# The list of tokens read as one run per partition, its places worked out on VectorE

## The reference

```
x = x + cross_attention(layernorm(x), ctx)          # 1 head: own key and 77 outer keys
h = layernorm(x)
qkv  = h @ W_qkv + b_qkv                             # 16 heads of 32
attn = softmax(q k^T / sqrt(32)) v
gate = softmax(h @ W_gate + b_gate)                  # 8 experts
top_g, top_i = top_k(gate, 2)                        # two experts for each token
moe  = sum over the two of  top_g * (h @ W_experts[e] + b_experts[e])
x = x + attn + moe
```

## Time and profile before

| | us |
|---|---|
| median of 3 runs | 1365.55 |
| lowest, highest | 1362.95, 1366.89 |
| the profiled execution | 1362.68 |
| its span | 1361.0 |

### The profile page before, as it was taken

The page is one execution under the profiler, slowest core; times in us unless marked ns, Lnnn a source line. Parts: engine busy times, 40 slices in busy tenths (PEclk is TensorE's granted clock), DMA queues, the critical chain, the costliest instruction groups (busy, mean ns, idle before and its releaser), DMA issues.

```text
span 1361.0 us, 27015 instructions
## 1 busy us (share of the span) xinstructions
PE 1252.1 (92%) x7540; PEld 961.7 (71%) x7541; DVE 960.1 (71%) x2149; ACT 893.8 (66%) x1874; POOL 373.4 (27%) x580
## 2 busy tenths in 40 slices
PE   5928999999888899999999999999996999999997
PEld 4927888888666567767777677777774666787775
DVE  5517888888678888888888888888885673433332
ACT  3303444444348789999999999999995783334332
POOL 0002222222200011310213102130005174667775
PEclk9878999999899999999999999999999898999999
DMA  5055777777665247455674555744559677887874
GB/s 185 14 171 176 277 259 252 267 261 254 237 171 137 60 135 171 86 126 140 159 170 85 125 138 153 179 83 127 134 122 251 243 188 185 242 190 131 143 139 59
DMA packets 114301, 225.28 MB, mean 166 GB/s; under 512 B 27627, under 2 KB 35963, under 8 KB 111941
## 3 DMA queue, kind: packets, MB, share of 16 engines
q1 hardware_dynamic: 86517, 181.76, 44.4%
q0 software_dynamic: 26624, 42.04, 17.2%
q10 hardware_dynamic: 1104, 0.81, 0.2%
HBM read 89.72 MB, written 77.75 MB: 123 GB/s over the span
## 4 chain that ended last, share of the span: by engine, by line
PE 72%; DVE 7%; DMA 7%; ACT 5%; issue 4%; SPq 3%; another core or an unknown queue 1%; POOL 1%; POOLq 1%; DVEq 0%; ACTq 0%
PE banks L237 14%; PE banks L239 13%; PE banks L238 13%; PE banks L1241 8%; PE banks L1222 8%; PE banks L1200 7%; DMA out_dram<-plain,score_bias 4%; ACT plain L928 2%; ACT banks L921 2%; DVE plain L1761 2%; SPq L417 2%; PE banks L1330 1%; PE banks L1070 1%; PE banks L1108 1%
## 5 line engine op out<-in xcount | busy, mean ns | idle before, releaser
L237 PE MATMUL banks<-parts 128*128 128x512 f32 (+8 forms) x1036 | 418.4, 404 | 29.7 <-DVE parts L1542 7.4
L239 PE MATMUL banks<-parts 128*128 128x512 f32 (+8 forms) x1036 | 398.4, 385 | 0.0
L238 PE MATMUL banks<-parts 128*128 128x512 f32 (+8 forms) x1036 | 397.9, 384 | 0.0
L1761 DVE TENSOR_REDUCE plain<-banks 128x1 f32<-128x512 f32 x512 | 339.9, 687 | 72.8 <-PE banks L1200 54.8
L921 ACT ACTIVATE banks<-banks,plain 128x512 f32<-128x512 f32 x512 | 345.1, 679 | 15.5 <-DVE plain L1761 15.2
L928 ACT ACTIVATE plain<-banks 128x1024 f32<-128x1024 f32 x256 | 265.8, 1038 | 45.7 <-PE banks L1222 40.4
L237 PEld LDWEIGHTS banks<-parts 128*128 128x128 f32 (+2 forms) x1036 | 198.9, 192 | 79.0 <-issue 18.3
L239 PEld LDWEIGHTS banks<-parts 128*128 128x128 f32 (+2 forms) x1036 | 197.6, 191 | 39.1
L238 PEld LDWEIGHTS banks<-parts 128*128 128x128 f32 (+2 forms) x1036 | 199.0, 192 | 28.6
L1200 PE MATMUL banks<-parts 96*128 96x512 f32 x512 | 181.2, 405 | 0.2 <-issue 0.2
L1222 PE MATMUL banks<-parts 104*128 104x512 f32 x512 | 176.0, 425 | 2.6 <-ACT plain L928 2.6
(11 more groups left out here) (193 smaller groups left out, 1532.0 us busy)
## 6 DMA issues: line engine op xcount, KB each, us to landing
parts<-parts SPq DMA_DIRECT2D x385, 128.0 KB, 2.4
parts<-h_turned SPq DMA_DIRECT2D x46, 512.0 KB, 6.2
experts_split<-parts SPq DMA_DIRECT2D x32, 512.0 KB, 4.1
h_turned<-parts SPq DMA_DIRECT2D x32, 512.0 KB, 2.9
parts<-experts_split SPq DMA_DIRECT2D x8, 2048.0 KB, 9.1
plain<-in_x_dram SPq DMA_DIRECT2D x32, 256.0 KB, 4.1
plain<-in_L_ffn_W_experts_dram SPq DMA_DIRECT2D x32, 256.0 KB, 4.2
out_dram<-plain SPq DMA_DIRECT2D x32, 256.0 KB, 2.8
```

The source lines that it names most:

```text
L237: pe.matmul(out, stat[0], mov[0], start=first, stop=False)
L238: pe.matmul(out, stat[0], mov[1], start=False, stop=False)
L239: return pe.matmul(out, stat[1], mov[0], start=False, stop=last)
L1761: dve.tensor_reduce(nmx[:, k, t:t + 1], bank[SB[t]][:], AX.X, ALU.max, negate=True).then_inc(q["f_max"], 1)
```

## The change

Memory holds the list by partition now: entry p of block i is at p * 72 + i rather than at i * 128 + p. The read is then one run of 576 bytes for each partition. So that the scatters write there, VectorE turns each place s into the new one: i = s >> 7, and 72 s + (1 - 128 * 72) i = 72 (s - 128 i) + i. The first fill of the list writes the same number to all places and stays as it is. What lies in `lst` afterwards is the same as before.

```
@@ read_list
-                sp.dma_start(lst, slot_dram.rearrange("(i p) c -> p i c", p=P)).then_inc(q["in_list"], 16)
+                sp.dma_start(lst, slot_dram.rearrange("(p i) c -> p i c", p=P)).then_inc(q["in_list"], 16)
@@ choice_records
                 then(dve.tensor_reduce(mx, t_eq, AX.X, ALU.add))
-                then(dve.tensor_copy(rec[:, a, :, 0].bitcast(U32), mx))
+                slot = rec[:, a, :, 0].bitcast(U32)
+                then(dve.tensor_copy(slot, mx))
+                then(dve.tensor_scalar(slot, slot, 7, None, ALU.logical_shift_right))
+                then(dve.tensor_copy(den, slot))
+                then(dve.tensor_scalar(mx, mx, float(NB), None, ALU.mult))
+                then(dve.scalar_tensor_tensor(out=slot, in0=den, scalar=float(1 - P * NB), in1=mx, op0=ALU.mult, op1=ALU.add))
                 then(dve.tensor_copy(rec[:, a, :, 2], gates[a]))
```

## The result

| | before, us | changed, us |
|---|---|---|
| median of 20 runs each | 1362.57 | 1365.43 |
| lowest, highest | 1358.24, 1366.89 | 1362.93, 1369.82 |
| the profiled execution | 1362.68 | 1363.53 |
| its span | 1361.0 | 1361.9 |

The ratio of changed to before is 1.0024, with a 95% interval of 1.0015 to 1.0034: **3.3 us slower** by the ratio (2.9 by the medians), within the 0.3% that I had called the same. The forecast was 2.2 us faster, also "the same", and its range, 1356 to 1370, holds the time. That is partly luck: the forecast time stood on a median of 3 runs (1365.55), and by 20 runs the kernel before takes 1362.57, 3.0 us less. As a difference the forecast is off by 5.1 us. The change went the other way than forecast, and the interval leaves no doubt on that. So the sum has to be taken apart.

What follows compares the result with a forecast made beforehand. PE's matmul work was 72% of the chain, with batch 0's routing and the last batch's start as places to weigh. 1362.68 + 1.8 - 4.0 = 1360.5 us profiled, 1363.3 us as median; range 1356 to 1370.

Steps and rivals of the forecast that it cites:

- The price of the eight instructions: Batch 0, near 445 and 452 us: eight added VectorE instructions at 0.225 us each, 1.8 us more.
- Their effect on the path: Batch 0: nothing covers the added instructions and no later idle time gives back their 1.8 us.
- The removed packets: Start of the last batch: 9,216 packets of 8 bytes go, freeing nearly the whole 4.1 us of queue time.
- can go out some 2.4 us earlier: SP's queue, last batch: bias row and six stack transfers leave 2.4 us earlier, not 3.8, as stacks await VectorE's R1.
- That the first fetch doesn't start sooner: GpSimd, last batch: line 654 ran until 0.6 us after the list landed, so an earlier list starts no fetch sooner.
- What of the read lies on the path: Last batch: chain gaps with no releaser in the trace (13.4 us) follow DMA backlog; gain 4.0 us, bounds 0 to 11.7.
- the read is hidden and stays hidden: Last batch: fetches begin at the same moment, no engine waits for the list; only VectorE's 1.8 us remain: 1367.4; chance 0.20.
- The rival with a new stall: Last batch: second eight fetches begin 4 us earlier and meet other transfers; a further 8.1 us stall, +5.9: 1371.5; chance 0.13.
- The rival in which the longest stall goes: Last batch: expert and stacks clear before the fetches, the 8.11 us stall and low clock go, -9.9: 1355.7; chance 0.17.
- The sum of the gaps: Last batch: gaps without releaser come earlier with about the same sum; forecast wrong if not between 9 and 14 us.
- The other sign: Last batch: forecast wrong if the first heads' end does not move by what the DMA engines were relieved of.

Runs made afterwards that it cites:

- e1: Kernel before plus the eight VectorE instructions writing to a place nobody reads, old read kept; 1357.51 us, ratio 1.0023 to before.
- c_after_third: The changed kernel run a third time, on the fourth chip, without gaps, against the kernel before; 1350.62 us, ratio 0.9979.
- c_after: The changed kernel repeated on the second chip, with gaps, against the kernel before; 1367.24 us, ratio 1.0023.
- c_before: The kernel before, unchanged, run again on the second chip for another profile; 1364.39 us, ratio 1.0002.
- e5: Kernel before with the old read put ahead of the copy of V on SP; 1363.64 us, ratio 1.0002.
- e9: Kernel before with only fetches 0 to 2 up front in the last batch, the others behind the first three weighings; 1352.40 us, ratio 0.9998.
- e10: Kernel before with only fetches 0 to 2 up front and the old read ahead of V's copy; 1345.30 us (0.9942) without gaps, 1348.67 us (0.9898) with.
- c_after_again: The changed kernel run again on the third chip, with gaps, against the kernel before; 1366.92 us, ratio 1.0028.
- e7: Kernel before with GpSimd's second eight fetches put off to between the first weighings; 1355.56 us (0.9949), repeated 1356.21 us (0.9948).
- e3: Kernel before with the old read done twice, one behind the other, the second waited for by nobody; 1349.52 us, ratio 0.9961.

## Why the prediction was wrong, point by point

**The price of the eight instructions: right.** 1.8 us, from the neighbouring rows, and 0.18 to 0.20 us each in the trace. That they count in full was right as well.

**Their effect on the path: the term that was mis-sized.** I wrote that nothing gives the 1.8 us back and looked no further. But it was 3.5 to 4.2 us in every kernel with all eight instructions behind heads 7 and 8 (the three repetitions, the result's profile and e1). Of what is missing, 1.7 us is one fall of PE's granted clock behind the wait that grew from 1.36 to 2.25 us. The Trainium skill, "TensorE: Matmul & The Clock Gate", section Terms, puts the penalty at the throttled time times the missing share of the clock; 3.4 us at one half gives an estimated 1.7 us, and the shift in `c_after_third` (1.84 to 3.5) agrees. With it alone the sum would have been 1362.68 + 3.9 - 4.0, no change.

**The removed packets: right in the transfer, wrong in who profits.** The read landed in 4.6 us instead of 9.5 (4.9 less, where I had 4.1) and SP's hold went from 4.75 to 0.35. That the stacks "can go out some 2.4 us earlier" was wrong: 8.62 us against 8.60 behind the copy of V. I had named the hold of SP's queue and VectorE's R1 as their waits and left out the third, PE's turned scores (line 1222), which end 0.03 to 0.04 us before they go out in both kernels.

**That the first fetch doesn't start sooner: right.** Line 654 and the fetch kept their places (1031.03 and 1032.61, both shifted like the copy of V before them).

**What of the read lies on the path: the step that failed most.** I tied the 4.1 us to the gaps without releaser and let the path follow the backlog. Where there are gaps the relief in the stretch was 0.7 us (`c_after` against `c_before`) and 1.1 in e5, of which its median shows nothing. The rival "the read is hidden and stays hidden" was the right one for them; with 3.9 us in batch 0 rather than 1.8, and the 0.7 taken off, it gives 3.2 us, and the result was 3.3. That it fits to 0.1 us is luck: both terms come from single profiles, in which the time behind the stretch scatters by 7 us. On two chips without gaps the read was on the path by a route that I had seen and not followed: the rows of the first block. I wrote that the block "landed only by 1042.2, 13 us after its issue", and did not ask when PE would need them. In the trace of before PE reached them at 1043.2, since the gaps had delayed it. Take the gaps away, and PE is there 4 us too early. There the relief is 5.4 us in the stretch (7.1 by the medians of e9 and e10) and the change is 2.7 us faster.

The Trainium skill, "DMA: Bandwidth & Descriptors", Rules for kernel authors, says that a transfer issued early and waited for late overlaps with compute. I had weighed this for the list. The runs agree for the list and show its limit: what was hidden was the list's own time, not the 2 MB and the rows queued behind it.

**The rival with a new stall** did not occur: the gaps of `c_after` add up to 13.7 us and those of `c_after_again` to 12.9, where before had 13.4. **The rival in which the longest stall goes** named the right prize and the wrong key: it goes with GpSimd's second eight fetches (e7), not with the read.

**The signs I had asked for.** The sum of the gaps is between 9 and 14 us in the two repetitions with gaps, as said, but 6.8 in the result's own profile (entries "issue"), so that there this sign spoke against the forecast. The other sign was that the time at which the first heads of the last batch end "does not move by what the DMA engines were relieved of", and it is what came in the repetition: 0.7 against 4.1.

**What stays open.** What the gaps are. They stand in all twelve profiles of the chips of the result and of the second, third and last table (in the one of the changed kernel as "issue"), and in none of the seven of the first and fourth. The longest needs the second eight fetches at their early place (e7), and neither the read's place (e5) nor its form makes the gaps. No trace names what they wait for. That they belong to the chip is likely but rests on few: only one chip (the third) was used twice, and it had them both times. And the time behind the stretch, 290 to 297 us over the nineteen profiles, was not looked into.

## What to carry to other kernels

A wait that grows by a microsecond on a busy TensorE is to be priced with the clock behind it: look at the granted clock around the place, and add half the length of one low stretch, if falls stand near. When a transfer gets shorter, ask what stands behind it in the queue and when its consumer arrives, and do the sum once more with the stalls of today taken away: they may hide the very wait that the change removes. And where a gain hangs on two or three microseconds at one crowded place, reordering the transfers there (late fetches later, the small one first) is worth more than making one of them cheaper: e10 is 15.0 us faster than before on a chip with gaps and 8.0 on one without, the change 3.9 slower and 2.7 faster on the same two.

## What the runs showed of the hardware

**Chips differ, and with them the sign of a change.** The kernel before has medians of 1354.9 and 1353.3 us on two chips, of 1364.0 on a third and of 1363.1 and 1363.7 on a fourth. The kernel before was profiled on the slower ones alone, but e1, with the same read and fetches, shows the place on a faster one: its stretch is 30.9 us against 40.2. The same changed kernel is 2.7 us faster on one and 3.3 and 3.9 us slower on others, each with an interval that does not hold 1.

**A copy of 72 KB in 8-byte pieces moved at 21 GB/s** The earlier trace rows and cost its queue 4.1 us, and still less than its place did: doubled, it made the kernel 5.4 us faster (e3), as I read it by holding back 2 MB. With nothing ahead of it, it landed in 7.3 us (e5) and 7.2 (e10), behind the copy of V in 9.5.

**The low clock moves about.** From 440 to 500 us the kernel before has one fall of some 3.4 us, near 476. `c_after_third` has none there, and its shift stays at 3.5 us across the place: that fall costs nothing. Its own one, as long, stands at 456 and costs 1.7 us. The place decides the price.
